# Six extra products of 256 columns a step on TensorE, ahead of the wait for exponentials, in the two filling slots that have scores

## The chip, the cores and the metric

The kernel runs on one core of one Trainium2 chip. The metric is the device time of one execution in microseconds. The engines are named as in the profile: PE is TensorE, DVE is VectorE, ACT is ScalarE, POOL is GpSimd, SP is SyncE, which here only issues DMAs.

## The reference

A transformer block with layer norm ahead of each half, over x of 32 sequences x 256 tokens x 128 channels, all fp32. First attention with 16 heads of 8 channels, local in windows of 64: each query sees the 64 keys up to its own. Then a mixture of 16 experts (hidden size 64, four chosen per token, by groups) beside one shared expert of size 128.

```python
x = x + _L0_attn_ref(_layernorm(x, axis=-1), Wq, Wk, Wv, Wo)
x = x + _L0_ffn_ref(_layernorm(x, axis=-1), gate_kernel, gate_bias, w_gate, w_up, w_down, ...)
...
base = (j > i) & (j <= i + W)
scores = jnp.where(mask, einsum(q, k2) * scale, -1e+30)
out = einsum(softmax(scores), v2)
```

## The kernel before

The tokens are cut into 16 groups of 512 (two sequences each). A group passes through a pipeline by hand: every stage has a number (SC = 8 for its first scores, FF = 28 for its first expert pair, YE = 37 for its output), and a slot has eight steps, so that stage n of group g runs in slot g + n // 8 at step n % 8. Slots 0 to 3 are written out, slots 4 to 15 are a loop over pairs of slots, and slots 16 to 19 drain the pipeline. `filling(slot)` holds for slots 0 to 2. The order of each engine's work within a step is the order in which the code of that engine's block is written; the engines meet by counting semaphores only.

In a step of slot 1 or 2, TensorE does first the products into the shared banks that have the place EARLY (values, VP, and the logits of routing, LG), then the expert products `gate_up` (from slot 3 on), then the scores of one unit u of the group that entered a slot ago. A unit's scores fill two banks, one for each half of the rows (`rows` 0 and 1). `hide` (L845) puts the mask there by a product of a bf16 band with an identity, and `scores` (L857) adds the products of q_by_head and k_by_row. VectorE then takes the row maxima (`neg_max`, L736), and ScalarE the exponentials (`probs`, L579), four for each half. In a filling slot TensorE waits for each half apart: it may write half `rows` again when the exponentials of this half from the step before are done (semaphore s_p, "probs_ready"). In the later slots it waits once for both.

Behind the scores, in the same step, come what else is due: products of the transposed probabilities with the values (L940, PV, in two steps out of four), transposes of the attention output (L953, L960), the output projection (L970), the projections Q and K (L819 to L821, three products each, from values split in a high and a low part, float32r), and the transposes of the normalised input X (L1024). The normalisation runs on GpSimd (L515 to L522) behind the statistics that VectorE takes at step 3 (L644). Bank 7 of PSUM collects the output of the experts, first in slot 3 (`start=True` at the first product).

Of the kernel before, what the change touches and what calls it, by code (L numbers as in the profile page):

```python
# [13 lines left out]
P = 128  # L14
# [16 lines left out]
NU = NSB // 2  # L31
# [13 lines left out]
SC = 8  # L45
# [33 lines left out]
def at(slot, s, stage, stride=1, count=1):  # L79

    for k in range(count):
        d = stage + k * stride
        if d % STEPS == s:
            off = d // STEPS
            if slot.fixed and not 0 <= slot.n - off < NG:
                return None, 0
            return Group(slot.n - off, (slot.par + off) % 2, slot.fixed), k
    return None, 0
# [22 lines left out]
def filling(slot):  # L111

    return slot.fixed and slot.n < 3
# [37 lines left out]
WQ, WK, WV, WO, GK = 0, C, 2 * C, 3 * C, 4 * C  # L151
# [2 lines left out]
W_COLS = WU + NF * P  # L154
LOADS, FFN_LOADS = 4, 6
PREPARE = 4
ORDER_PER_SLOT = 5
ROUTING_DVE, ROUTING_POOL = 8, 5
NO_SCORE, GROUP_IN = -3.0e38, 2.0 ** 60
# [2 lines left out]
def preln_block_kernel(nc, x, w_att, gate_b, w_gu, w_down, sw_down, consts, out):  # L162
    with ExitStack() as ctx:
        def sb(name, shape, dt=F32):
            return ctx.enter_context(nc.sbuf_tensor(name, shape, dt))
# [6 lines left out]
        w_hi = sb("w_hi", [P, W_COLS], F32R)  # L172
# [74 lines left out]
        PS = ctx.enter_context(nc.psum_tensor("PS", [P, 8, 512], F32))  # L247
# [174 lines left out]
        def _(pool):  # L422
# [8 lines left out]
            def slot(sl):  # L431
                for s in range(STEPS):
                    if sl.fixed and sl.n == 1 and s == PREPARE:
                        pool.wait_ge(s_wf, 16 * FFN_LOADS)
# [187 lines left out]
        def _(dve):  # L622
# [3 lines left out]
            def link(sl, ins):  # L626

                order["done"] += 1
                ins.then_inc(s_dve, 1)
                loop = 0 if sl.fixed else (sl.n - LOOP_FIRST) * ORDER_PER_SLOT  # L630
                dve.wait_ge(s_dve, order["before"] + loop + order["done"])
# [63 lines left out]
            def slot(sl):  # L695
# [109 lines left out]
                else:  # L805
                    assert order["done"] == ORDER_PER_SLOT, order["done"]
                    if sl.par == 1:
                        order["before"] += (LOOP_END - LOOP_FIRST) * ORDER_PER_SLOT

# [4 lines left out]
        def _(pe):  # L814
            mm = nc.tensor.matmul
# [47 lines left out]
            def slot(sl):  # L863
                for s in range(STEPS):
# [9 lines left out]
                    g, _ = at(sl, s, VP)  # L874
# [4 lines left out]
                    g, _ = at(sl, s, LG)  # L879
                    if g:  # L880
# [7 lines left out]
                                         *w2(GK, E))  # L888
                        ins.then_inc(s_filled[side], 1)

                    g, k = at(sl, s, FF, 1, NP)
                    if g:
                        gate_up(g, k)
# [29 lines left out]
                    for turn_, stage in enumerate(PV):  # L923
                        g, _ = at(sl, s, stage)
# [10 lines left out]
                        for kb in range(4 * later, 4 * later + 4):  # L935
                            nq = min(3, NQ - kb)
                            for a in range(HG):
# [5 lines left out]
                                         start=(kb == 0 and a < 2), stop=(kb == NQ - 1), skip_group_check=True)  # L943
# [28 lines left out]
                    g, _ = at(sl, s, SH)  # L972
# [6 lines left out]
                    g, _ = at(sl, s, QP)  # L979
# [4 lines left out]
                    g, _ = at(sl, s, KP)  # L984
# [11 lines left out]
                    if g:  # L996
# [8 lines left out]
                        for n in range(NT):  # L1005
                            r = slice(P * n, P * n + P)
                            ins = mm(PS[:, 7, r], hh[:, k % 2, r], wd[:, k, :], start=(k == 0 and n == 0),  # L1007
                                     stop=(k == NP - 1), skip_group_check=True)
                        if k == NP - 1:
                            ins.then_inc(s_dn, 1)  # L1010
                    g, _ = at(sl, s, CT)
# [7 lines left out]
                    g, _ = at(sl, s, XT)  # L1019
                    if g:  # L1020
# [4 lines left out]
                        ins.then_inc(s_filled[side], 1)  # L1025

            run_slots(pe, slot)


# [45 lines left out]
```

## Time and profile before

| | |
|---|---|
| median of 3 runs | 743.44 us |
| lowest, highest | 741.68, 744.17 us |
| the profiled execution's own time | 743.04 us |
| its span, first to last instruction | 741.1 us |
| TensorE busy | 695.4 us (94%) |
| weight loads busy | 568.0 us |
| ScalarE, VectorE, GpSimd busy | 535.5, 508.4, 454.1 us |
| mean granted TensorE clock | 0.985 |

The span is that of one profiled execution; its own time is 1.94 us longer. Weight loads (PEld) run beside the products of the same engine. The granted clock is the share of full clock that TensorE was given, as the chip's events record it.

### The profile page before, as it was taken

Reading aid. Unit: us, or ns where it says so; the run is one execution under the profiler, and the core shown is the slowest. Engines: PE = TensorE matmul, PEld = TensorE weight load, DVE = VectorE, ACT = ScalarE, POOL = GpSimd, SP = SyncE. Lnnn points to the kernel's source line nnn. Section 1 sums busy time; section 2 is a strip of 40 time slices with the busy share of each in tenths; the row PEclk is TensorE's granted clock in tenths of the full one; section 3 lists DMA queues with packets and bytes.
Section 4 is the critical chain, followed back from the end, with each engine's and each line's share of the span. In section 5 each row is a group of like instructions: output and inputs, shape, how many; then the busy total and the mean of one; then the engine's idle time right before and its main releaser. Section 6 shows DMA issues by size and latency. Waiting matters only on the chain.

```text
span 741.1 us, 19372 instructions
## 1 busy us (share of the span) xinstructions
PE 695.4 (94%) x6264; PEld 568.0 (77%) x6264; DVE 508.4 (69%) x1588; ACT 535.5 (72%) x1603; POOL 454.1 (61%) x561
## 2 busy tenths in 40 slices
PE   3778889999999999999999999999999999999997
PEld 1667668888887878788787878788888878778775
DVE  2456585868677685867677685867768585876564
ACT  3675778787777878787878779787877878764332
POOL 6233156767777676767767676767767576445433
PEclk9998899999999999999999999999999999999999
DMA  5010013040413123040313113040313213041321
GB/s 167 1 30 11 20 62 99 28 130 20 127 45 115 57 72 100 17 129 26 117 54 114 58 60 112 5 138 28 115 57 102 69 50 108 3 128 32 115 73 43
DMA packets 50243, 52.58 MB, mean 71 GB/s; under 512 B 5664, under 2 KB 31904, under 8 KB 50080
## 3 DMA queue, kind: packets, MB, share of 16 engines
q1 hardware_dynamic: 50208, 52.14, 22.7%
q8 instruction: 19, 0.31, 0.2%
q14 instruction: 16, 0.13, 0.1%
HBM read 43.20 MB, written 4.72 MB: 65 GB/s over the span
## 4 chain that ended last, share of the span: by engine, by line
PE 75%; ACT 9%; DVE 9%; issue 4%; DMA 1%; POOL 1%; DVEq 0%; POOLq 0%; ACTq 0%; SPq 0%
PE PS L940 11%; PE PS L1007 11%; PE PS L819 11%; PE PS L857 10%; PE PS L821 10%; PE PS L820 10%; ACT probs L579 5%; PE PS L845 3%; PE PS L970 3%; DVE neg_max L736 2%; PE PS L953 2%; DVE tu L728 2%; PE PS L1004 2%; PE PS L1024 1%; ACT q_by_head L531 1%
## 5 line engine op out<-in xcount | busy, mean ns | idle before, releaser
L579 ACT ACTIVATE probs<-PS,neg_max 128x96 f32<-128x96 f32 (+1 forms) x1024 | 247.3, 350 | 90.9 <-DVE neg_max L736 90.9
L460 POOL TENSOR_TENSOR gate<-gate,spread 128x512 f32<-128x512 f32 x124 | 158.6, 1279 | 166.4 <-ACT gate L531 88.8
L728 DVE SCALAR_TENSOR_TENSOR tu<-th,PS 128x512 f32<-128x512 f32 x128 | 87.5, 683 | 100.9 <-ACT th L547 70.9
L1007 PE MATMUL PS<-wd,hh 128*128 128x128 f32 x1024 | 136.4, 276 | 4.4 <-DVE hh L788 2.2
L736 DVE TENSOR_REDUCE neg_max<-PS 128x4 f32<-128x384 f32 (+1 forms) x256 | 122.3, 516 | 21.6 <-PE PS L857 17.0
L1007 PEld LDWEIGHTS PS<-wd,hh 128*128 128x128 f32 x1024 | 126.8, 192 | 12.1 <-DVE hh L788 4.9
L465 POOL TENSOR_TENSOR hh<-gate,tu 128x512 f32<-128x512 f32 x100 | 127.9, 1279 | 7.8
L819 PE MATMUL PS<-x_hi,w_hi 128*128 128x512 f32 x288 | 124.6, 433 | 0.2 <-DVE tu L728 0.2
L821 PE MATMUL PS<-x_lo,w_hi 128*128 128x512 f32 x288 | 114.4, 397 | 0.0
L714 DVE STREAM_TRANSPOSE probsT<-probs 128x768 f32<-128x768 f32 (+1 forms) x128 | 114.4, 893 | 0.0
L857 PE MATMUL PS<-k_by_row,q_by_head 64*128 64x192 f32 (+2 forms) x1024 | 113.9, 327 | 0.0
L820 PE MATMUL PS<-x_hi,w_lo 128*128 128x512 f32 x288 | 113.5, 394 | 0.0
L547 ACT ACTIVATE th<-PS 128x512 f32<-128x512 f32 x128 | 79.9, 624 | 44.0 <-PE PS L821 42.4
L940 PE MATMUL PS<-probsT,v_bd 128*64 128x96 f32 (+2 forms) x2048 | 96.4, 250 | 0.9 <-DVE probsT L714 0.9
L940 PEld LDWEIGHTS PS<-probsT,v_bd 128*64 128x64 f32 x2048 | 86.5, 142 | 12.8 <-issue 7.9
L857 PEld LDWEIGHTS PS<-k_by_row,q_by_head 64*128 64x128 f32 x1024 | 89.5, 197 | 0.0
L531 ACT ACTIVATE gate<-PS 128x512 f32<-128x512 f32 x128 | 79.9, 624 | 0.0
L845 PEld LDWEIGHTS PS<-band,ident 64*128 64x128 bf16 x320 | 14.5, 94 | 66.1 <-issue 32.0
L821 PEld LDWEIGHTS PS<-x_lo,w_hi 128*128 128x128 f32 x288 | 54.2, 188 | 12.3
L819 PEld LDWEIGHTS PS<-x_hi,w_hi 128*128 128x128 f32 x288 | 54.6, 190 | 8.6 <-DVE tu L728 0.4
L820 PEld LDWEIGHTS PS<-x_hi,w_lo 128*128 128x128 f32 x288 | 54.7, 190 | 7.5
L845 PE MATMUL PS<-band,ident 64*128 64x256 bf16 (+2 forms) x320 | 40.1, 256 | 18.1 <-ACT probs L579 16.6
(106 smaller groups left out, 963.7 us busy)
## 6 DMA issues: line engine op xcount, KB each, us to landing
spread<-weights_by_expert SPq DMA_DIRECT2D x248, 128.0 KB, 2.9
X<-x SPq DMA_DIRECT2D x32, 256.0 KB, 3.2
OUT<-H SPq DMA_DIRECT2D x16, 256.0 KB, 3.1
out<-OUT SPq DMA_DIRECT2D x16, 256.0 KB, 2.9
ffn_stage<-w_gu SPq DMA_DIRECT2D x1, 1152.0 KB, 5.7
wd<-w_down SPq DMA_DIRECT2D x1, 512.0 KB, 6.6
weights_by_expert<-cT SPq DMA_DIRECT2D x16, 32.0 KB, 1.6
probsT<-w_att SPq DMA_DIRECT2D x1, 192.0 KB, 2.7
```

What stands on the lines that cost most here:

```text
L460: tt(gate2[:, :], gate[:, k % 2, :], spread[:, k % SP_BUFS, :], ALU.mult).then_inc(s_g2, 1)
L465: tt(hh[:, k % 2, :], gate2[:, :], tu[:, k % 2, :], ALU.mult).then_inc(s_h, 1)
L579: ins = nc.scalar.activation(probs[:, u % 2, tt, 2 * rows + e, j0:KW], PS[:, rows, n * KW + j0:n * KW + KW], ACT.Exp, bias=neg_max[:, rows ...
L714: v_.transpose(probsT[:, b, :, t0:t0 + 2, c0:3, :].rearrange("p g t c q -> p t g (c q)"), probs[:, u % 2, :, :, c0 * Q:KW]).then_inc(s_pt, 1)
L728: v_.scalar_tensor_tensor(tu[:, k % 2, :], th[:, :], 1.0, PS[:, 5, :], ALU.add, ALU.mult).then_inc(s_tu, 1)
L736: v_.tensor_reduce(neg_max[:, rows, :], src[:, :, j0:KW], AX_X, ALU.max, negate=True).then_inc(s_m, 1)
L819: mm(dst, l_hi, r_hi, start=True, stop=False)
L820: mm(dst, l_lo, r_hi, start=False, stop=False)
L821: return mm(dst, l_hi, r_lo, start=False, stop=True)
L857: ins = mm(dst[:, :, KW - nk:KW], q_by_head[r, g.par, q1 // Q - 1, :, :].rearrange("p v q -> p (v q)"), k_by_row[r, g.par, :, q1 - nk:q1], ...
L940: ins = mm(PS[r0:r0 + 64, 2, c0:c0 + Q * nq], v_bd[:, g.par, b * NQ + kb, a, :, :].rearrange("p k f -> p (k f)"), pt[:, 3 * kb + 2:3 * kb ...
L1007: ins = mm(PS[:, 7, r], hh[:, k % 2, r], wd[:, k, :], start=(k == 0 and n == 0), stop=(k == NP - 1), skip_group_check=True)
```

## The change

A constant BUSY = 6 is added, and in TensorE's block, between the routing logits and `gate_up`, a loop of six products for every step in which the slot is a filling one and a group has scores. These are slots 1 and 2, all eight steps, so 96 products. Each takes 128 columns of w_hi (the query weights) as the stationary operand and the 256 columns of query and key weights as the moving one, and writes 128x256 of bank 7. Nothing reads the result. No semaphore is waited for or raised.

```diff
 PREPARE = 4
+BUSY = 6
 ORDER_PER_SLOT = 5
...
                         ins.then_inc(s_filled[side], 1)
 
+                    if filling(sl) and at(sl, s, SC, 1, NU)[0]:
+                        for _ in range(BUSY):
+                            mm(PS[:, 7, 0:WV], w_hi[:, WQ:WQ + P], w_hi[:, WQ:WV], start=True, stop=True)
+
                     g, k = at(sl, s, FF, 1, NP)
                     if g:
                         gate_up(g, k)
```

TensorE at the end of step 0 and in step 1 of slot 1, before the change (the names in brackets are semaphores waited for):

```order
L857 MATMUL PS<-k_by_row,q_by_head 128x2x32
L857 MATMUL PS<-k_by_row,q_by_head 128x2x64
L845 MATMUL PS<-band,ident 128x4x2x32 [waits probs_ready]
L857 MATMUL PS<-k_by_row,q_by_head 128x192 x2
L845 MATMUL PS<-band,ident 128x4x2x32 [waits probs_ready]
L857 MATMUL PS<-k_by_row,q_by_head 128x192 x2
```

The same place in the changed kernel, where lines ahead of the loop have a number higher by one (L857 is L858) and lines behind it higher by five (L940 is L945):

```order
L858 MATMUL PS<-k_by_row,q_by_head 128x2x32
L858 MATMUL PS<-k_by_row,q_by_head 128x2x64
L894 MATMUL PS<-w_hi 128x256 x6
L846 MATMUL PS<-band,ident 128x4x2x32 [waits probs_ready]
L858 MATMUL PS<-k_by_row,q_by_head 128x192 x2
L846 MATMUL PS<-band,ident 128x4x2x32 [waits probs_ready]
L858 MATMUL PS<-k_by_row,q_by_head 128x192 x2
```

The six products (L894) stand between the last score product of step 0 and the first wait of step 1 for probs_ready.

TensorE at the end of step 0 and in step 1 of slot 2, where the output projection (L970) comes between, before the change:

```order
L940 MATMUL PS<-probsT,v_bd 64x96 x15
L970 MATMUL PS<-wo,oT 128x128 [waits ffn_weights_loaded,shared1_taken,shared0_taken]
L970 MATMUL PS<-wo,oT 128x128
L845 MATMUL PS<-band,ident 128x4x2x32 [waits probs_ready]
L857 MATMUL PS<-k_by_row,q_by_head 128x192 x2
L845 MATMUL PS<-band,ident 128x4x2x32 [waits probs_ready]
L857 MATMUL PS<-k_by_row,q_by_head 128x192 x2
L940 MATMUL PS<-probsT,v_bd 64x96 [waits probsT_ready]
L940 MATMUL PS<-probsT,v_bd 64x96 x7
L940 MATMUL PS<-probsT,v_bd 64x64 x4
```

And in the changed kernel:

```order
L945 MATMUL PS<-probsT,v_bd 64x96 x15
L975 MATMUL PS<-wo,oT 128x128 [waits ffn_weights_loaded,shared1_taken,shared0_taken]
L975 MATMUL PS<-wo,oT 128x128
L894 MATMUL PS<-w_hi 128x256 x6
L846 MATMUL PS<-band,ident 128x4x2x32 [waits probs_ready]
L858 MATMUL PS<-k_by_row,q_by_head 128x192 x2
L846 MATMUL PS<-band,ident 128x4x2x32 [waits probs_ready]
L858 MATMUL PS<-k_by_row,q_by_head 128x192 x2
L945 MATMUL PS<-probsT,v_bd 64x96 [waits probsT_ready]
L945 MATMUL PS<-probsT,v_bd 64x96 x7
```

Here the six products stand behind the output projection and ahead of the scores of step 1; the probability products (L940, now L945) of that step come behind them.

## Rows read from the trace of the kernel before

**Rows 1.** The page: busy time and share by engine, and the granted clock in tenths.
```profile
PE 695.4 (94%) x6264; PEld 568.0 (77%) x6264; DVE 508.4 (69%) x1588; ACT 535.5 (72%) x1603; POOL 454.1 (61%) x561
...
PEclk9998899999999999999999999999999999999999
```

**Rows 2.** Windows: stretch, its length, busy PE, PEld, DVE, ACT, POOL, clock, DMA, GB/s.
```profile
0.00:84.00 84.00, 58.82 (x440) 46.08 (x440) 41.88 (x104) 52.32 (x168) 29.64 (x37) 0.92 0.17 50
...
110.00:740.00 630.00, 614.25 (x5589) 504.37 (x5588) 447.06 (x1408) 465.48 (x1378) 414.46 (x506) 1.00 0.24 75
...
50.20:53.60 3.40, 3.40 (x36) 3.16 (x36) 0.43 (x1) 3.32 (x11) 0.00 (x0) 0.53 0.03 7
...
64.30:67.00 2.70, 2.70 (x24) 2.26 (x24) 1.56 (x3) 1.64 (x9) 2.51 (x4) 0.50 0.00 0
```

**Rows 3.** Timeline of TensorE: start, length, engine, line, operation, shapes, count.
```profile
12.78 0.63 PE L820 MATMUL PS<-xT_hi,w_lo 128*128 128x512 f32 x1
13.21 0.63 PE L821 MATMUL PS<-xT_lo,w_hi 128*128 128x512 f32 x1
...
39.91 0.39 PE L821 MATMUL PS<-xT_lo,w_hi 128*128 128x512 f32 x1
40.14 0.39 PE L819 MATMUL PS<-xT_hi,w_hi 128*128 128x512 f32 x1
...
82.99 0.26 PE L820 MATMUL PS<-w_hi,x_lo 128*128 128x16 f32 x1
83.11 0.26 PE L821 MATMUL PS<-w_lo,x_hi 128*128 128x16 f32 x1
```

**Rows 4.** Timeline of all engines, two steps of slot 1.
```profile
24.44 0.39 PE L845 MATMUL PS<-band,ident 64*128 64x256 bf16 x1 [0.90 <-ACT probs L579]
...
26.15 0.56 DVE L736 TENSOR_REDUCE neg_max<-PS 128x4 f32<-128x384 f32 x1 [1.40 <-PE PS L857]
...
27.89 0.39 PE L845 MATMUL PS<-band,ident 64*128 64x256 bf16 x1 [0.86 <-ACT probs L579]
```

**Rows 5.** Timeline of all engines, two steps of slot 2.
```profile
56.98 0.28 PE L845 MATMUL PS<-band,ident 64*128 64x256 bf16 x1 [0.26 <-ACT probs L579]
...
57.95 0.56 DVE L736 TENSOR_REDUCE neg_max<-PS 128x4 f32<-128x384 f32 x1 [0.42 <-PE PS L857]
...
59.69 0.28 PE L845 MATMUL PS<-band,ident 64*128 64x256 bf16 x1 [0.27 <-ACT probs L579]
```

**Rows 6.** Timeline of TensorE: longer waits, in brackets with what ended them.
```profile
18.23 0.32 PE L845 MATMUL PS<-band,ident 64*128 64x128 bf16 x2 [1.45 <-ACT k_by_row L531]
...
21.04 0.39 PE L845 MATMUL PS<-band,ident 64*128 64x256 bf16 x1 [1.31 <-ACT probs L579]
...
44.01 0.65 PE L953 MATMUL PS<-cst,o_f 128*128 128x128 f32 x4 [1.87 <-ACT q_by_head L531]
...
48.66 0.24 PE L845 MATMUL PS<-band,ident 64*128 64x128 bf16 x2 [1.49 <-ACT probs L579]
```

**Rows 7.** Timeline: end of group 1's normalisation on GpSimd, and X's transposes.
```profile
34.67 1.04 POOL L522 TENSOR_TENSOR X<-X,rs 128x512 f32<-128x512 f32 x1
...
36.31 0.86 PE L1024 MATMUL PS<-cst,X 128*128 128x128 f32 x4
```

**Rows 8.** Chain that ended last: start, length, engine, tile, line, count.
```profile
50.28 2.60 PE PS L940 x32
52.89 1.13 PE PS L970 x4
...
65.88 2.76 PE PS L940 x32
68.63 1.15 PE PS L970 x4
...
71.74 1.25 PE PS L940 x32
...
105.00 0.64 PE PS L970 x4
```

## The prediction

> **What bounds the kernel now.** I first read the page: TensorE is busy for 94% of the span and no other engine for more than 72% [rows 1]. Then I read the busy time in three stretches: from 110 us on TensorE works 614.25 of 630 us at full granted clock, but only 58.82 of the first 84 us [rows 2]. So the loop is bound by TensorE, and a microsecond won or lost while the pipeline fills moves everything behind it by that microsecond. The change touches only slots 1 and 2, which lie between about 17 and 84 us.
>
> Next I read the clock. The row of tenths shows falls in that part [rows 1], and two windows make them exact: granted 0.53 in 50.2 to 53.6 us and 0.50 in 64.3 to 67.0 us [rows 2]. A third such stretch is short, around 77.5 to 81 us. For the first 33 us the row says 9 or more, but the products say otherwise: two products of 512 columns start 13.21 - 12.78 = 0.43 us apart, which is 1.2 columns a nanosecond, the level of 1.2 GHz; at 40 us the same pair is 0.23 us apart, the level of 2.4 GHz [rows 3]. The same slow spacing of the score products holds until about 36 us. I therefore take the clock as low from the start to about 36 us. The Trainium skill ("TensorE: Matmul & The Clock Gate", section "Seeing it yourself") warns that recorded clock events have been seen to be unreliable and are to be checked against something else. By the column the saving in slot 1 below (1.8 us) would not exist and the sum would come out at -2.0 us; by the spacing it does, and I go by the spacing.
>
> What a step costs at either clock is in the timeline. Low: hiding products at 24.44, first row maxima at 26.15, next step at 27.89, so 3.45 us [rows 4]. High: 56.98, 57.95, 59.69, so 2.71 us [rows 5]. The whole difference, 0.74 us, is TensorE's (1.71 against 0.97 us until the maxima can start); VectorE and ScalarE take the same. TensorE idles ahead of each wait for exponentials: 0.90 and 0.86 us in the low steps, 0.26 and 0.27 us in the high ones. Longer gaps are 1.87 us at 44.01 and 1.49 us at 48.66 [rows 6], and one like the latter just before the stretch at 64 us. Each of the two long low stretches of slot 2 begins behind such a gap of about 1.5 us.
>
> **What the change adds.** 16 groups of six products (both slots, eight steps), each 128x256 from resident weights, into a bank first needed in slot 3; no semaphore, no wait, no DMA. They stand on TensorE behind the early uses of the shared banks and before the wait for exponentials; all later work of TensorE queues behind them. No trace row has this shape. Bounds at the high clock: products of 16 columns with a full weight load start 0.12 us apart and those of 512 columns 0.23 us [rows 3], so six take 0.72 to 1.38 us; half of the 512-column spacing is just under 0.12, so I take 0.12 x 6 = 0.7 us. At the low clock half of 0.43, 0.215 x 6 = 1.29 us. The same page of the Trainium skill gives, in "Back-to-back issue gap", columns / 2.4 + 2.5 ns for isolated products, an estimate of 0.66 us for six; with it the sum below would gain some 0.2 us more. For 512 columns it would say 0.216 us where the trace has 0.23, so I stay with the rows.
>
> **What it may bring: the clock.** With 1.29 us of products, the gaps of 0.9 us in the low steps vanish, and TensorE works without pause from 15 us on. In the trace the clock rose after dense stretches without such gaps (33.5 to 37 us, and 50.2 to 53.6 us, busy 3.40 of 3.40 us [rows 2]) and fell behind the 1.5 us gaps. I expect the rise to come at the first or second step of slot 1 (20 to 24 us), not at 36, and the falls at 50, 64 and 77 us not to come, since 0.7 of 1.5 us is filled. That is an inference from few events.
>
> **The sum**, against the profiled run:
>
> Slot 1. Step 0's products fit in the 1.45 us that TensorE waits for k_by_row; step 1's fit its 1.31 us [rows 6]. Steps 2 and 3 begin with the clock high: steps 1 to 3 save 0.74 us each at most, and the layer-norm statistics behind step 3's maxima come about 1.4 us sooner (the step before and half of its own). GpSimd's chain behind them ends at 34.67 + 1.04 = 35.71, so at 34.3; TensorE's transposes of X, at 36.31 because the low-clock probability products stood in front of them [rows 7], start at 34.35. Gain 2.0 us. Step 5's products stand right behind them, 0.7 us, of which 0.5 lie beside the split of xT on ScalarE and VectorE: 1.8 us are left. Step 6's products go beside the 1.87 us wait for q_by_head [rows 6] and cost nothing. Step 7's stand behind the K projection with no gap: +0.7. Slot 2 begins 1.1 us earlier.
>
> Slot 2. Step 0's products lie in the 1.49 us gap [rows 6]: nothing. The probability products then take 1.25 instead of 2.60 us and the output projection 0.64 instead of 1.13 [rows 8]: -1.8, so -2.9. Step 1's products (0.7) stand before the scores; the transpose of probabilities on VectorE (0.97 us) covers most, but TensorE has its next products behind them, and with step 2's (0.7 against a gap of 0.26 [rows 5]) the lead at step 2 is -1.9. Step 3: gap 0.27, so +0.4, -1.5. Step 4: gap as at 48.66, nothing. Then the second long low stretch: 2.76 becomes 1.25, 1.15 becomes 0.64 [rows 8], half a step of scores saves 0.5, the transposes of X 0.2: -2.7, but GpSimd's xn1 is then late by 0.4: -3.8. Step 5's products +0.7 less 0.3 that the scores save at the high clock: -3.4. Step 6: hidden beside q_by_head. Step 7: +0.7; the three K products at 0.23 instead of 0.43 us give 0.6, the transposes before them 0.15, the scores 0.3: -3.8.
>
> Slot 3 has no such products and I leave its two low stretches as they are. So the span is 741.1 - 3.8 = 737.3 us. The profiled execution took 743.04 us, 0.4 us below the median of 743.44, and 1.9 us lie around its span: 739.2 us for it, **739.6 us** against the median. A change under 0.3%, 2.2 us, can't be told from none.
>
> **Rivals.** (1) The clock rises early, but one or two of the falls in slot 2 still come: with the second long stretch low, 2.7 us are lost and step 5's products cost 0.6 more, -3.8 + 3.3 = -0.5; with only the first low, about -1.7. So 741.5 to 744.5 us. For it: only half of each 1.5 us gap is filled, and dense products of few columns left the clock low from 64.3 to 67.0 us although TensorE was busy throughout [rows 2]. Chance 0.22.
> (2) The other side: the clock stays where it is, and the products are pure work. Exposed: steps 2 to 4 of slot 1 0.4 each (1.29 less 0.9), step 5 0.5, step 7 0.7; in slot 2 step 1 0.85 (low clock, less the cover of VectorE's transpose), steps 2 and 3 0.45 each, step 5 1.0, step 7 1.29: 6.4 us, 749.8 us. With the rise in slot 1 alone it is 4.0 less 1.1, +2.9, 746.3 us. It is decided where the maxima of steps 2 to 4 still come 1.7 us after the step's start. Together 0.14. The Trainium skill (same page, section "What's actually happening") says that low is the default and that activity releases it, which speaks against the first half of this rival; no row here shows what the chip counts.
> (3) More than I sum: the phase shifts so that slot 3's low stretches (probability products of 2.7 us at 85.5 us, and one at 98 us) also go, worth 1.4 and 0.8 us: 737.4 us. For it only that a filled pipeline may start slot 3 tighter. Chance 0.08.
> My forecast has 0.56.
>
> **How the numbers follow.** The forecast alone runs from 738 (the rise a step sooner, products at the page's price) to 741.5 (the rise two steps later, 1.5 us; or products at 0.23 us each, 0.66 more in each of the six exposed groups, which would take all of it to 743). Faster by over 0.3% (under 741.2): the forecast without its edge, rival 3, and the better end of rival 1: 0.66. Within: the rest of rival 1 and the edges, 0.21. Slower: rival 2, 0.13. The range takes in rival 3 in part and the lower form of rival 2 in part: 736.8 to 745.8 us.
>
> **What the profile after should show.** The six products 0.215 us apart in steps 0 and 1 and about 0.12 us from then on; score steps of slot 1 of 2.7 us; transposes of X near 34.3 us; granted clock 1.00 from 45 to 84 us; slot 3's first products near 79 us instead of 82.9 us; the loop the same length as before. Wrong would be: low clock anywhere in slot 2, products spaced 0.2 us at the high clock, or a loop that gives the gain back because it was not TensorE but a wait across slots that set its pace.

## Result, and the profile after

The changed kernel takes 736.83 us (median of 6 runs, 735.67 to 737.95), the kernel before 742.50 us in the runs beside it. The ratio is 0.992 (95% interval 0.9904 to 0.9936): 5.7 us faster, where the prediction said 3.8 us. The profiled execution took 735.67 us, the fastest of the six, with a span of 733.8 us against 741.1 us. Three of the six had a mean granted clock of 0.997 and three of 0.993, against 0.985 in the profiled execution before. These means are to be read with care: the record of the clock does not always begin at the start (see the run of slot 2 alone below), and executions of the kernel before with 0.970 to 0.974 took 741.84 to 743.76 us, no longer than those with 0.985.

The page of the changed kernel, the lines that answer to [rows 1] and the row of instruction loads:

```profile
PE 694.9 (95%) x6360; PEld 569.5 (78%) x6360; DVE 508.9 (69%) x1588; ACT 534.0 (73%) x1603; POOL 453.3 (62%) x561
...
PEclk9999999999999999999999999999999999999999
...
q8 instruction: 20, 0.33, 0.2%
```

The slices with an 8 are gone. Windows of the changed kernel (columns as in [rows 2]) over the two stretches that were low in slot 2, over the start of slot 3, and over the one stretch that is left:

```profile
50.00:53.60 3.60, 3.60 (x54) 3.20 (x54) 2.83 (x9) 2.46 (x9) 0.00 (x0) 1.00 0.00 0
62.00:67.00 5.00, 4.62 (x60) 4.07 (x60) 2.95 (x6) 2.34 (x9) 2.79 (x3) 1.00 0.00 0
78.00:84.00 6.00, 5.53 (x87) 4.79 (x88) 3.17 (x8) 5.36 (x19) 0.96 (x4) 1.00 0.01 4
90.50:94.00 3.50, 3.30 (x19) 2.23 (x20) 3.01 (x8) 1.46 (x7) 0.57 (x2) 0.59 0.00 0
```

The timeline of TensorE in the changed kernel, at the places of [rows 4] to [rows 7]:

```profile
16.67 1.49 PE L894 MATMUL PS<-w_hi 128*128 128x256 f32 x6
...
19.61 0.98 PE L894 MATMUL PS<-w_hi 128*128 128x256 f32 x6
...
24.04 0.28 PE L846 MATMUL PS<-band,ident 64*128 64x256 bf16 x1 [0.30 <-ACT probs L580]
...
26.75 0.28 PE L846 MATMUL PS<-band,ident 64*128 64x256 bf16 x1
...
33.97 0.63 PE L1029 MATMUL PS<-cst,X 128*128 128x128 f32 x4 [1.02 <-POOL X L523]
...
41.79 0.66 PE L958 MATMUL PS<-cst,o_f 128*128 128x128 f32 x4 [0.94 <-ACT q_by_head L532]
...
46.70 0.24 PE L846 MATMUL PS<-band,ident 64*128 64x128 bf16 x2 [0.78 <-ACT probs L580]
...
54.22 0.28 PE L846 MATMUL PS<-band,ident 64*128 64x256 bf16 x1
...
54.70 0.28 PE L846 MATMUL PS<-band,ident 64*128 64x256 bf16 x1
...
56.93 0.28 PE L846 MATMUL PS<-band,ident 64*128 64x256 bf16 x1
...
57.85 0.28 PE L846 MATMUL PS<-band,ident 64*128 64x256 bf16 x1
...
77.46 0.25 PE L820 MATMUL PS<-w_hi,x_hi 128*128 128x16 f32 x1 [1.03 <-ACT oT L532]
...
79.61 1.54 PE L945 MATMUL PS<-probsT,v_bd 128*64 128x96 f32 x32
...
90.66 0.28 PE L846 MATMUL PS<-band,ident 64*128 64x256 bf16 x2 [2.11 <-ACT probs L580]
```

The first group of six takes 1.49 us to its end, the second 0.98: the clock has risen by then, near 19.5 us, although the granted clock reads 1.00 throughout. The steps of slot 1 take 26.75 - 24.04 = 2.71 us instead of 3.45. The gap at the start of slot 2 is 0.78 instead of 1.49 us [rows 6], and no fall follows it. The probability products of slot 3 take 1.54 us; before they took 2.74, in a low stretch at 85.5 us. The one fall that is left follows the wait of 2.11 us at 90.66, where there are no extra products.

Where the time went, as the start of the same work in both traces (us): first scores of slot 2, 48.66 and 46.70 (-2.0); scores of step 2, 56.98 and 54.22 (-2.8); routing logits of slot 3, 82.89 and 77.46 (-5.4); first down products (L1007, now L1012), 110.52 and 103.51 (-7.0); end of span -7.3. The loop gives nothing back. Of the 7.3 us of this execution 5.4 come in the slots that the change touches and 1.6 in slot 3, between the logits and the first down products.

### The profile page after: what moved, and what is told of

It reads as the page before. It is cut to its first block, busy times and chain, and to the rows that moved or that the text cites. A ratio compares the mean times of both kernels' runs of the same rounds, so it can differ in the third digit from the quotient of the medians.

```text
span 733.8 us, 19564 instructions
## 1 busy us (share of the span) xinstructions
PE 694.9 (95%) x6360; PEld 569.5 (78%) x6360; DVE 508.9 (69%) x1588; ACT 534.0 (73%) x1603; POOL 453.3 (62%) x561
## 4 chain that ended last, share of the span: by engine, by line
PE 74%; ACT 9%; DVE 9%; issue 4%; POOL 2%; DMA 1%; DVEq 0%; POOLq 0%; ACTq 0%; SPq 0%
PE PS L1012 11%; PE PS L820 11%; PE PS L945 10%; PE PS L822 10%; PE PS L821 10%; PE PS L858 9%; ACT probs L580 5%; PE PS L846 3%; PE PS L975 3%; PE PS L958 2%; DVE neg_max L737 2%; PE PS L1009 2%; DVE tu L729 2%; ACT q_by_head L532 1%; PE PS L1029 1%
## 5 line engine op out<-in xcount | busy, mean ns | idle before, releaser
L1012 PE MATMUL PS<-wd,hh 128*128 128x128 f32 x1024 | 136.4, 276 | 4.3 <-DVE hh L789 2.2
L1012 PEld LDWEIGHTS PS<-wd,hh 128*128 128x128 f32 x1024 | 126.8, 192 | 12.1 <-DVE hh L789 4.9
L858 PE MATMUL PS<-k_by_row,q_by_head 64*128 64x192 f32 (+2 forms) x1024 | 108.0, 317 | 0.0
L945 PE MATMUL PS<-probsT,v_bd 128*64 128x96 f32 (+2 forms) x2048 | 91.5, 242 | 0.5 <-DVE probsT L715 0.5
L945 PEld LDWEIGHTS PS<-probsT,v_bd 128*64 128x64 f32 x2048 | 82.0, 137 | 12.1 <-issue 7.6
L858 PEld LDWEIGHTS PS<-k_by_row,q_by_head 64*128 64x128 f32 x1024 | 84.1, 190 | 0.0
L846 PE MATMUL PS<-band,ident 64*128 64x256 bf16 (+2 forms) x320 | 38.6, 251 | 12.2 <-ACT probs L580 11.7
```

What stands on the lines that cost most here:

```text
L858: ins = mm(dst[:, :, KW - nk:KW], q_by_head[r, g.par, q1 // Q - 1, :, :].rearrange("p v q -> p (v q)"), k_by_row[r, g.par, :, q1 - nk:q1], ...
L945: ins = mm(PS[r0:r0 + 64, 2, c0:c0 + Q * nq], v_bd[:, g.par, b * NQ + kb, a, :, :].rearrange("p k f -> p (k f)"), pt[:, 3 * kb + 2:3 * kb ...
```

## The experiments

**How the runs are padded.** The first four showed something that had to be removed before the rest could be read: three of them came out 16 to 20 us slower than the kernel before, and the loss lay in the loop, which no edit touched. The run p1 below shows why. Later runs therefore carry padding where their number of products differs from the change's: waits on a count that is long reached, two to an instruction, at the start of TensorE's program (192 of them raise the page's count from 19372 to 19468 instructions). A product with its weight load is two instructions, so the change puts 192 instructions ahead of the loop. The expectations count in bytes, 64 to an instruction, a size that no trace here shows; nothing below hangs on it. "Loop as in the changed kernel" means 192 instructions (12288 bytes) beyond the kernel before, or that plus 256 (16384 bytes).

**Slot 1 alone, unpadded.**

```diff
-                    if filling(sl) and at(sl, s, SC, 1, NU)[0]:
+                    if sl.fixed and sl.n == 1 and at(sl, s, SC, 1, NU)[0]:
```

> The six products only in the eight steps of slot 1. Theory (the gain is the clock's, each slot apart): the clock rises near 19.5 us as with the whole change, slot 2 begins near 46.7 us instead of 48.7, and then the falls near 50, 64 and 77 us come back; about 2 us faster than before, 740.5 us. Rival (once the clock is high early it stays high by itself, slot 2's products are pure cost): low time gone in slot 2 as well, 736 us or less.

Measured: 762.3 us, ratio 1.024 (1.020 to 1.028). Neither theory. Up to the first down products, at 107.20 us, this kernel is 3.3 us ahead of the one before (110.52); the loss comes in the loop. Its page and its waits of TensorE between 120 and 640 us (waits, times, longest):

```profile
q8 instruction: 64, 1.05, 0.6%
...
PE PS L820 <- issue: 10.2, 5, 2.4
```

64 packets of instruction loads instead of 19 before and 20 in the changed kernel, and five stalls of TensorE at the same line, one for each time that the loop starts again: nine more packets at each, 1.05 MB / 64 = 16 KB a packet. Around one of them the clock falls too:

```profile
201.70:203.50 1.80, 0.08 (x1) 0.00 (x0) 1.00 (x2) 1.80 (x8) 1.21 (x1) 1.00 0.24 62
203.50:207.00 3.50, 3.44 (x17) 3.06 (x18) 0.00 (x0) 1.46 (x4) 0.00 (x0) 0.69 0.43 155
```

**Slot 2 alone, unpadded** (`sl.n == 2` in the same place).

> The six products only in the eight steps of slot 2. Theory: slot 1 as before (low clock to about 36 us, slot 2 begins at 48.7 us), no fall in slot 2, about 3.7 us faster than before, 738.8 us. Rival (slot 2's gain needs the early rise, or most of the gain is slot 1's): under 2 us faster, with a low stretch in slot 2.

Measured: 759.58 us, ratio 1.023 (1.019 to 1.027), with the same 64 packets, so outside both expectations. Up to the loop it is ahead: first down products at 107.92 us, by 2.6 us. Its windows of 17 to 36 and 63 to 74 us:

```profile
17.00:36.00 19.00, 14.19 (x87) 11.96 (x87) 9.24 (x23) 12.56 (x46) 3.77 (x6) 0.52 0.00 1
63.00:74.00 11.00, 10.86 (x113) 9.51 (x114) 6.91 (x21) 6.06 (x24) 4.87 (x8) 0.84 0.15 49
```

This execution's record of the clock begins early enough to say 0.52 for slot 1, what the spacing of the products [rows 3] had said of the kernel before against its column of 1.00. The second row is a miss: I had expected no fall in slot 2, and with its products in place one came (0.84).

**Sixteen columns.**

```diff
-                            mm(PS[:, 7, 0:WV], w_hi[:, WQ:WQ + P], w_hi[:, WQ:WV], start=True, stop=True)
+                            mm(PS[:, 7, 0:16], w_hi[:, WQ:WQ + P], w_hi[:, WQ:WQ + 16], start=True, stop=True)
```

> As the change, but each of the 96 products moves 16 columns instead of 256: the same number of instructions and weight loads. Theory (it is the work of the array that raises the clock): the score steps of slot 1 still take 3.4 us, low stretches in slot 2 remain, 742 to 744.5 us. Rival (any instructions on TensorE that fill the wait would do, or it is only that its queue stays primed): 737 to 739 us, and the clock as with the whole change.

Measured: 745.54 us, ratio 1.0031 (1.0016 to 1.0046), loop as in the changed kernel, 20 packets. The program has the instructions of the changed kernel one for one. Its timeline and windows:

```profile
23.67 1.45 PE L894 MATMUL PS<-w_hi 128*128 128x16 f32 x6
...
25.05 0.39 PE L846 MATMUL PS<-band,ident 64*128 64x256 bf16 x1
...
28.55 0.39 PE L846 MATMUL PS<-band,ident 64*128 64x256 bf16 x1
...
32.41 0.34 PE L846 MATMUL PS<-band,ident 64*128 64x128 bf16 x2
```

```profile
50.00:54.00 4.00, 4.00 (x39) 3.55 (x39) 0.74 (x2) 3.93 (x12) 0.00 (x0) 0.50 0.01 2
```

The steps take 3.50 and 3.86 us, none has idle ahead of it any more, and slot 2 has its low stretch. Six of these narrow products take 1.45 us at the low clock, as long as six wide ones (1.49 us at 16.67 us in the changed kernel), so the wait is filled for as long. Filling it with instructions brings nothing; the gain is the clock's, and narrow products in the same number and over the same time did not raise it. The time is 1 us above the expected range.

**Twelve products** (`BUSY = 12`).

> Twelve products a step instead of six. Theory: the clock is high all the same; six more cost 0.71 us a step, of which the idle left in five steps of the changed kernel (0.5 to 0.9 us each) takes about 3.5 of 11.4: 7 to 8 us slower than the changed kernel, 744 to 745 us. Rival (products ahead of a wait are mostly hidden, because the gaps are wider than the rows of idle say): 2 to 4 us slower, 739 to 741 us.

Measured: 763.74 us, ratio 1.028 (1.024 to 1.032), 65 packets: the loop again. The expected price is to be read from the padded run below.

**The kernel before, with padding alone.**

```diff
+            for _ in range(192):
+                pe.wait_ge(s_pool, 1)
             pe.wait_ge(s_w, 16 * LOADS)
```

> The kernel before, with 96 instructions of padding (192 waits on a count that is long there) at the start of TensorE's program, where TensorE has nothing to do yet, so that its loop lies 6144 bytes further on, as in the runs of one slot only. Theory (the 16 to 20 us of those runs came from where TensorE's loop lies in its program, with about 64 packets of instruction loads instead of 19): 757 to 764 us. Rival (they came from the products themselves): 742.5 us, within 0.3% of before.

Measured: 765.54 us, ratio 1.0276 (1.024 to 1.031), 1.5 us beyond the theory's range and far from the rival. Page and waits of TensorE between 120 and 640 us:

```profile
q8 instruction: 64, 1.05, 0.6%
...
PE PS L819 <- issue: 10.6, 5, 2.3
```

No product was added, and the loss is there. 3.0 us of it are the padding itself, which holds the first transposes back from 8.35 to 11.35 us; the run of slot 1 alone, padded (below), has the same delay and no loss in the loop. What decides is not settled: 0, 192 and 448 instructions beyond the kernel before (0, 12288 and 28672 bytes) load 19 to 21 packets, 96 and 384 (6144 and 24576 bytes) load 64 or 65. It is shown that the position of TensorE's loop decides, not by which rule.

**Slot 1 alone and slot 2 alone, padded** (the edits above with 96 instructions of padding).

> The six products in slot 1 alone, with 96 instructions of padding at the start, so that TensorE's loop lies where it does in the changed kernel. The unpadded run reached slot 3's routing logits at 79.85 us and the first down products at 107.20, against 82.89 and 110.52 before. Theory (the loop has the same length as before once it lies there): 3.0 to 3.5 us faster than before, 739 to 740.5 us. Rival: over 750 us.

> The six products in slot 2 alone, padded in the same way. The unpadded run reached the same two places at 80.57 and 107.92 us. Theory: 2.3 to 2.7 us faster than before, 740 to 741 us; with slot 1 alone it makes about the 5.7 us of the whole change, so the two parts add. Rival: over 750 us.

Measured: slot 1 alone 742.17 us, ratio 0.9975 (0.9964 to 0.9985); slot 2 alone 743.22 us, 0.9998 (0.9986 to 1.0009). Both are outside what I expected, and the loop is whole (20 packets each). The padding is again what I had not priced. First scores of slot 1 in the two:

```profile
21.23 0.32 PE L848 MATMUL PS<-band,ident 64*128 64x128 bf16 x2 [0.17 <-ACT k_by_row L532]
```
```profile
21.23 0.32 PE L848 MATMUL PS<-band,ident 64*128 64x128 bf16 x2 [1.45 <-ACT k_by_row L532]
```

21.23 instead of 18.32 us in the changed kernel: 2.9 us late through the padding. Without these 2.9 us the two would be at 739.3 and 740.3 us, 4.2 and 3.1 us faster than the 743.46 us of before in the runs beside them. The subtraction is mine, no run shows it, and it may be too small: at the first down products the traces are 3.4 us (slot 1, 110.62 us) and 4.0 us (slot 2, 111.92 us) behind the same edits without padding. The unpadded traces give 3.3 and 2.6 us of lead there, 5.9 together, against 7.0 of the whole change. So each slot is worth something like 3 us, and how far the two add is not settled.

Slot 1's high clock alone does not keep slot 2's: this run of slot 1 alone has a granted clock of 0.69 in 63 to 74 us. But slot 2's products do not keep it for certain either. The start of slot 2 with them in place:

```profile
51.22 0.24 PE L848 MATMUL PS<-band,ident 64*128 64x128 bf16 x2 [0.78 <-ACT probs L580]
...
53.06 2.83 PE L947 MATMUL PS<-probsT,v_bd 128*64 128x96 f32 x32
```

The wait is the 0.78 us of the changed kernel, and the clock falls behind it all the same: 2.83 us where the changed kernel takes 1.54 (granted 0.50 in 52.7 to 55.8 us).

**Twelve products, padded** (64 instructions, done before the first transposes at 8.57 us).

> Twelve products a step, with 64 instructions of padding so that the loop lies as in the changed kernel. The unpadded run reached the two places at 82.50 and 112.01 us, 5.0 and 8.5 us behind the changed kernel. Theory: 743 to 745.5 us, since six more products cost 0.7 us a step and only about half of it is hidden. Rival (placement is not the cause): over 755 us.

Measured: 743.19 us, ratio 0.9993 (0.9983 to 1.0003), as expected. Six more products a step eat the whole gain, but not as work alone. 96 products x 0.12 us are 11.4 us of work; at the logits of slot 3 the trace is 5.2 us behind the changed kernel's (82.61 against 77.46). Up to the first down products it loses 3.5 us more (112.17 against 103.51), in slot 3, where neither kernel has such products: there the clock falls.

```profile
85.45 2.83 PE L947 MATMUL PS<-probsT,v_bd 128*64 128x96 f32 x32
```

In the medians the price of the six is 5.4 us by the ratios and 6.4 us by the times (743.19 - 736.83; the kernel before was 1 us slower beside these runs).

**Behind the wait.**

```diff
                                     pe.wait_ge(s_p, 2 * (g.n * NU + u) + rows - 1)
+                                if rows == 0:
+                                    for _ in range(BUSY):
+                                        mm(PS[:, 7, 0:WV], w_hi[:, WQ:WQ + P], w_hi[:, WQ:WV], start=True, stop=True)
```

> The same 96 products, but each six directly behind the first wait for exponentials of a step instead of ahead of it; the loop lies as in the changed kernel. Theory (the place ahead of the wait hides most of the products' own time, and they also fill the gap that lets the clock fall): the gaps stay, each step's maxima come 0.7 us later, so 8 to 11 us slower than the changed kernel, 745 to 748 us, with at least one low stretch in slot 2. Rival (only the amount of work counts for the clock and the place hardly matters): within 2 us of the changed kernel.

Measured: 748.91 us, ratio 1.0078 (1.0047 to 1.0109), about 12 us slower than the changed kernel with the same work and loop. Timeline of TensorE and the window of slot 2's first steps:

```profile
27.92 1.65 PE L917 MATMUL PS<-w_hi 128*128 128x256 f32 x6 [1.52 <-ACT probs L580]
```
```profile
54.00:63.00 9.00, 7.51 (x76) 6.38 (x78) 4.05 (x8) 6.41 (x21) 0.00 (x0) 0.81 0.00 1
```

The gap stays (1.52 us), the clock is still low at 28 us, and it falls again in slot 2. The place ahead of the wait is what makes the products cheap and the clock rise early. This is a little worse than expected; in this trace the clock of slot 1 rises only behind 41 us, and its steps take 5.0 us up to there.

**Slot 3 too, and slot 0 too.** In the first, the condition is `(filling(sl) or sl.fixed and sl.n == 3 and s < 5)`. In the second, nine products of the same form stand before the first transposes and six each before the Q and the K projection of slot 0.

> The change, and six such products also in steps 0 to 4 of slot 3 (bank 7 is free until step 5), with 4 instructions of padding so that the loop lies a whole 16384 bytes further than before. Theory: the low stretch of slot 3 at 90.7 to 93.7 us goes, worth about 0.9 us; the products of steps 0, 1 and 4 have no gap of their own and cost up to 0.7 us each: 735.5 to 738 us, no clear difference from the changed kernel. Rival (clock falls are what is left in the fill, products are nearly free): 733 to 735 us.

> The change, and products of the same form in slot 0: nine before the first transposes (from the moment the query weights are there), six before the Q projection and six before the K projection, all in gaps of TensorE; 23 instructions of padding, loop 16384 bytes further than before. Theory: the clock rises before 13 us instead of near 19.5; K, values and the first scores run at the high clock, slot 1's first scores start about 1 us sooner: 735 to 736.2 us. Rival (the first 18 us are set by ScalarE, VectorE and GpSimd, or the padding delays the start): no difference from the changed kernel or slower.

Measured: slot 3 too 738.01 us, ratio 0.9933 (0.9909 to 0.9957); slot 0 too 736.60 us, 0.9906 (0.9884 to 0.9929). Neither can be told from the changed kernel; for slot 0 that is the rival, not the theory of 735 to 736.2 us. With slot 3 the granted clock is 1.00 from 84 to 110 us, and yet the first down products start at 104.14 instead of 103.51 us: the products cost what the clock gives. With slot 0 the clock is up by the Q projection (0.50 us for the product that took 0.76) and slot 1 starts at 17.09 us, but in the profiled execution falls came back, in slot 2 (0.88 in 62 to 74 us) and at the start of slot 3 (0.83 in 74 to 84 us).

**Nine groups of sixteen, alone and with slot 0.**

```diff
+GAPS = [(1, n) for n in (0, 1, 2, 3, 4, 6)] + [(2, n) for n in (0, 4, 6)]
...
-                    if filling(sl) and at(sl, s, SC, 1, NU)[0]:
+                    if sl.fixed and (sl.n, s) in GAPS:
```

> Six products only in the nine steps whose group lies beside a wait (steps 0 to 4 and 6 of slot 1, steps 0, 4 and 6 of slot 2); the seven groups that stand in the chain of the changed kernel (0.7 to 0.9 us each, 5.1 us in all) are gone, and 84 instructions of padding keep the loop where it lies in the changed kernel. Theory (these seven are paid for and the nine others keep the clock up): 3 to 5 us faster than the changed kernel, 732 to 734 us. Rival A (the seven are needed, the clock falls in slot 2 without them): 736 to 740 us with a low stretch before 84 us. Rival B (the seven cost nothing, something else follows them): no difference from 736.8 us though the clock stays high.

> The run of nine groups, and the 21 products in the gaps of slot 0, which made slot 1 begin 1.2 us sooner; 43 instructions of padding, loop as in the changed kernel. Theory: about 1 us faster than the nine groups alone, 731 to 733 us. Rival (an earlier start moves the waits of slot 2 against the clock and a fall comes back, as in the profiled run with slot 0): no gain on the nine groups.

Measured: 735.81 us, ratio 0.990 (0.9885 to 0.9915), and 735.66 us, 0.9889 (0.9869 to 0.9909). The change has 0.992 (0.9904 to 0.9936), so they are ahead by 1 to 2 us at a size that the intervals don't separate. With slot 0 the rival came: no gain on the nine groups alone. Chain of the changed kernel at three of the groups left out, and then the timeline of the nine-group kernel (line numbers higher) at the logits of slot 3 and at steps 2 and 3 of slot 2:

```profile
43.14 0.71 PE PS L894 x6
...
56.22 0.71 PE PS L894 x6
...
65.70 0.71 PE PS L894 x6
```
```profile
52.67 0.28 PE L849 MATMUL PS<-band,ident 64*128 64x256 bf16 x1 [0.25 <-ACT probs L581]
...
55.38 0.28 PE L849 MATMUL PS<-band,ident 64*128 64x256 bf16 x1 [0.27 <-ACT probs L581]
...
75.30 0.25 PE L821 MATMUL PS<-w_hi,x_hi 128*128 128x16 f32 x1 [0.98 <-ACT oT L533]
...
77.77 2.82 PE L951 MATMUL PS<-probsT,v_bd 128*64 128x96 f32 x32
```

The seven groups add to 5.2 us in the chain, but without them the logits start only 2.2 us earlier (75.30 against 77.46). Step 2 to step 3 takes 2.71 us with six products in it (54.22 to 56.93) and 2.71 us without (52.67 to 55.38). The chain names whoever was last; it does not say that the next in line was 0.7 us behind. And 0.7 us is all that is left at the first down products (102.83 against 103.51): a fall comes at the start of slot 3 (2.82 us for the probability products, which took 1.54 in the changed kernel). The expected 3 to 5 us were wrong, and so was rival B's "nothing".

**The falls in all the traces.** The 32 probability products of step 0 and of step 4 in slot 2, and of step 0 in slot 3, take 1.54 us where the clock stays high and 1.85 to 2.83 us where it falls:

| trace | slot 2, step 0 | slot 2, step 4 | slot 3, step 0 |
|---|---|---|---|
| before | 2.67 | 2.83 | 2.74 |
| before, padded | 2.83 | 2.71 | 2.83 |
| slot 1 alone; padded | 1.54; 1.54 | 2.83; 2.83 | 2.83; 2.45 |
| slot 2 alone; padded | 1.54; 2.83 | 2.00; 2.06 | 2.83; 2.83 |
| the change | 1.54 | 1.54 | 1.54 |
| slot 3 too | 1.54 | 1.54 | 1.54 |
| slot 0 too | 1.54 | 2.30 | 2.75 |
| nine groups; with slot 0 | 1.54; 2.53 | 1.54; 1.54 | 2.82; 2.83 |
| twelve; padded | 1.54; 1.54 | 1.54; 1.54 | 2.83; 2.83 |
| sixteen columns | 2.83 | 2.83 | 2.73 |
| behind the wait | 1.85 | 1.54 | 2.46 |

Without wide products in slot 2 step 4 is low every time; with six ahead of the wait it is low in three traces of seven, and step 0 in two of the seven. The waits in front do not tell the two apart: 0.78 us stands before a fall and before none, and in the traces of slot 1 alone the clock stayed high behind 1.49 us.

## What in the prediction held, and which step failed

The direction and the mechanism are shown: wide products ahead of the wait lift the clock early, and the time follows the clock. The low clock of slot 1, read from the spacing against the column, is in the record of the run with slot 2 alone (0.52). The clock rose at the second step (predicted 20 to 24, measured near 19.5 us), the score steps of slot 1 take 2.71 us as in [rows 5], slot 2 holds 1.00. That it is the clock and not the filled queue is shown by the sixteen columns; that the place ahead of the wait matters, by the products behind it. The price of six, 0.7 us at the high clock, was measured as 0.71. X's transposes were forecast at 34.35 and start at 33.97 us.

What the runs do not bear out is the reason given for slot 2, that the falls would not come "since 0.7 of 1.5 us is filled". They stayed away in the trace of the change, but with the same products and the same wait they came in others (the table above). The products make a fall in slot 2 rarer; what decides it is open.

The step that failed in size is the exposure of the products in the sum, which took each group's 0.7 us minus the idle ahead of it as paid, and behind it the sentence on slot 3. The lead in the trace, against the forecast's:

| place | forecast | measured |
|---|---|---|
| transposes before step 7 of slot 1 (44.01, 41.79) | -1.8 | -2.22 |
| start of slot 2 (48.66, 46.70) | -1.1 | -1.96 |
| step 2 of slot 2 (56.98, 54.22) | -1.9 | -2.76 |
| step 3 (59.69, 56.93) | -1.5 | -2.76 |
| step 4 (63.60, 60.83) | -1.5 | -2.77 |
| logits of slot 3 (82.89, 77.46) | -3.8 | -5.43 |
| first down products (110.52, 103.51) | -3.8 | -7.01 |

- "Step 7's stand behind the K projection with no gap: +0.7." The lead goes from -2.22 to -1.96: 0.26 us were paid.
- "Step 3: gap 0.27, so +0.4." The lead is -2.76 at step 2 and at step 3: nothing was paid.
- Step 7 of slot 2, "+0.7" less 1.05 for the clock, was to gain 0.35; the lead went from -4.59 (transposes at 77.37 and 72.78 us) to -5.43, a gain of 0.84. Here too some 0.5 us less was paid.
- Steps 0 to 2 of slot 2 came out as forecast, 0.8 us of gain, products and all. The rest of the excess, 0.4 us, was there before step 7 of slot 1: the lead grew from -1.86 at the Q projection (39.34, 37.48) to -2.22 at the wait for q_by_head, where the sum had "cost nothing". At step 5 of slot 2 0.3 us less was gained than forecast and at step 6 0.25 us more.

What absorbs a group is, by the traces, the second half of a step, which otherwise waits for its own exponentials. In step 2 of slot 2 the products make the start late, the exponentials are done by then, and the second hiding product follows the first after 0.48 us (54.22, 54.70); in step 3 it follows after 0.92 us (56.93, 57.85). So the transposes behind step 2's scores start 1.35 us after the step's start instead of 1.79 us (55.57 - 54.22 against 58.77 - 56.98), and step 3's group finds 0.95 us of room behind them (55.98 to 56.93), where it needs 0.7. In step 7 of slot 1 the second follows after 0.12 us instead of 0.58. That this is the whole of it was not tried apart.

The second failed step is "Slot 3 has no such products and I leave its two low stretches as they are". In the profiled execution rival 3 came on top of the forecast: the first low stretch of slot 3 is gone, and the lead grows from 5.4 to 7.0 us. I had given it 0.08. Nothing here explains it: the kernels with nine groups and with twelve products entered slot 3 with the clock high and much the same wait at the logits (0.98 and 1.03 us), and it fell; of all traces only the change's and that of slot 3 too are without this fall. The profiled execution is also the fastest of the six, so this is luck of that execution as far as is known. The median execution has gained 5.7 us and not 7.3; which stretch came in which, their traces are not there to tell. Slots 1 and 2 account for 1.6 us more than forecast in this trace; how the median's 1.9 us (5.7 against 3.8) divide between them and slot 3 is open.

Rival 1 (a fall returns in slot 2) did not come in the profiled run of the change, but it did in those of slot 1 alone, of slot 2 alone, of slot 0 too and of the nine groups with slot 0; a chance of 0.22 was not too much. Rival 2, the products as pure cost, is what the sixteen columns show: +2.3 us. Its price of 6.4 us was for wide products at the low clock, which no run has ahead of the wait. A rival was missing from the list altogether: that code added in front of a loop moves the loop. This change moved it by 192 instructions, to a place as good as the old one; by 96 instructions it would have cost some 20 us, as the padded kernel before did. That the place was a good one is luck too.

## What to carry to other kernels

Where an engine waits in a pipeline's fill and its clock is low, work that nobody needs can pay if it stands ahead of the wait and is wide enough to lift the clock; behind the wait the same products lost 12 us. It does not hold the clock for certain: look at several traces before a fall that stayed away is counted as won. Idle in front of a wait was a lower bound of what fits here, because a late start also removed waits further on in the step; and a share in the chain was an upper bound of what leaving the work out gave. Before a difference of a few us is put down to an edit in unrolled code, count the instruction loads and look for stalls at the loop's start: a padded kernel before is the control.

## What was not expected of the hardware

- Padding alone, 96 instructions in front of TensorE's loop, made the kernel 22 us slower (765.54 against 743.46 us): 64 packets of instruction loads instead of 19, five stalls of some 2 us at the loop's start, and a clock of 0.98 over the loop. The change's own 192 instructions did no harm.
- 192 waits on a count long reached, 96 instructions, kept TensorE's first product back until 11.35 us; 128 waits were over before 8.57 us.
- A mean granted clock of 0.999 (slot 3 too) came with a longer time than 0.997 (the change): 736.57 and 735.67 us in the profiled executions.
- The granted clock read 1.00 in a stretch in which 512 columns took 0.43 us [rows 3]; in another kernel's trace the same stretch reads 0.52.
- The clock fell behind waits of TensorE of 0.75 and 0.78 us in some traces and stayed high behind 1.49 us in others, in the same steps of slot 2.
